# Banks for the maxima and the values, and the steps of the weight roundings, in a cross-attention stage

## The reference

```python
xn = _layernorm(x, ln1_w, ln1_b)              # ctx, 77 tokens, enters as the queries' side of the reference's names
q = latn @ Wq                                 # latents: 1024 tokens a batch, 16 heads of 64
kv = jnp.concatenate([xn, latn], axis=1) @ Wkv  # 77 + 1024 = 1101 keys and values
weight = jax.nn.softmax(einsum('bhld,bhnd->bhln', q * scale, k * scale), axis=-1)
out = einsum('bhln,bhnd->bhld', weight, v)    # then @ Wo, added to x
```

## Time and profile before

| | |
|---|---|
| runs of the kernel, median (lowest to highest) | 1946.68 us (1941.79 to 1953.57), 3 runs |
| the profiled execution, its own time | 1941.14 us |
| span of its trace, first to last instruction | 1939.4 us |
| granted TensorE clock, mean | 0.918 of full |
| TensorE busy | 1682.8 us |
| VectorE busy | 1233.6 us |
| GpSimd busy | 880.0 us |
| ScalarE busy | 698.5 us |

### The profile page before, as it was taken

The page is one execution under the profiler, slowest core; times in us unless marked ns, Lnnn a source line. Parts: engine busy times, 40 slices in busy tenths (PEclk is TensorE's granted clock), DMA queues, the critical chain, the costliest instruction groups (busy, mean ns, idle before and its releaser), DMA issues.

```text
span 1939.4 us, 46407 instructions
## 1 busy us (share of the span) xinstructions
PE 1682.8 (87%) x18226; PEld 1314.2 (68%) x18226; DVE 1233.6 (64%) x2531; ACT 698.5 (36%) x1295; POOL 880.0 (45%) x851
## 2 busy tenths in 40 slices
PE   1889999999998999999999727999999539999798
PEld 1677777777776777777777516777777425556587
DVE  8767767777775777767777742333675384346676
ACT  1344443444434344444444313444344201123122
POOL 4146655566551556655565524554454211112221
PEclk9899999999999999999999958999999756568699
DMA  8133433434421343443434191111211200000000
GB/s 202 34 88 87 121 92 86 99 87 121 102 77 33 90 99 87 121 97 81 99 91 112 41 394 59 59 51 45 73 40 32 77 0 1 1 1 1 33 12 33
DMA packets 67717, 148.43 MB, mean 77 GB/s; under 512 B 14779, under 2 KB 37619, under 8 KB 66996
## 3 DMA queue, kind: packets, MB, share of 16 engines
q1 hardware_dynamic: 63764, 135.20, 26.2%
q0 software_dynamic: 3744, 10.26, 1.4%
HBM read 57.85 MB, written 35.21 MB: 48 GB/s over the span
## 4 chain that ended last, share of the span: by engine, by line
PE 72%; DVE 13%; DMA 5%; issue 3%; ACT 2%; SPq 1%; POOL 1%; POOLq 0%; ACTq 0%; DVEq 0%
PE ps L1757 28%; PE ps L1853 9%; PE ps L1790 8%; PE ps L2020 7%; PE ps L1833 6%; PE ps L2110 6%; PE ps L1834 5%; DVE mxs L1203 4%; DMA KA<-K_l 4%; DVE Y L418 1%; SPq L585 1%; PE ps L1995 1%; PE ps L1860 1%; PE ps L2088 1%; DVE stats L399 1%
## 5 line engine op out<-in xcount | busy, mean ns | idle before, releaser
L756 POOL TENSOR_TENSOR PR<-PT 128x512 f16<-128x512 f32 (+1 forms) x416 | 441.6, 1073 | 442.1 <-ACT PT L966 441.9
L966 ACT ACTIVATE PT<-ps 128x512 f32<-128x512 f32 (+1 forms) x576 | 325.4, 596 | 382.9 <-PE ps L1834 382.8
L1853 PE MATMUL ps<-V_h,PT 128*128 128x65 f16 (+1 forms) x2304 | 319.8, 196 | 7.9 <-POOL PR L756 5.6
L1853 PE MATMUL ps<-V_l,PT 128*128 128x65 f16 (+1 forms) x2304 | 315.6, 194 | 0.0
L1853 PE MATMUL ps<-V_l,PR 128*128 128x65 f16 (+1 forms) x2304 | 314.0, 194 | 0.0
L1853 PE MATMUL ps<-V_h,PR 128*128 128x65 f16 (+1 forms) x2304 | 313.5, 193 | 0.0
L1203 DVE TENSOR_REDUCE mxs<-ps 128x1 f32<-128x736 f32 x256 | 236.2, 923 | 87.0 <-PE ps L1790 87.0
L1853 PEld LDWEIGHTS ps<-V_h,PT 128*128 128x128 bf16 (+1 forms) x2304 | 225.1, 98 | 97.9 <-issue 58.1
L1790 PE MATMUL ps<-KA,QA 128*128 128x368 f32 x768 | 214.6, 358 | 48.6 <-DVE mxs L1203 28.2
L1833 PE MATMUL ps<-QA,KA 128*128 128x512 f32 (+1 forms) x576 | 241.9, 420 | 15.6 <-ACT PT L966 10.8
L1834 PE MATMUL ps<-QB,KB 65*128 65x512 f32 (+1 forms) x576 | 229.2, 398 | 0.0
(11 more groups left out here) (354 smaller groups left out, 3745.6 us busy)
## 6 DMA issues: line engine op xcount, KB each, us to landing
QA<-Q_h SPq DMA_DIRECT2D x64, 256.0 KB, 4.6
latf<-wexp SPq DMA_DIRECT2D x32, 512.0 KB, 4.4
wsplit<-wst SPq DMA_DIRECT2D x32, 512.0 KB, 2.9
wx<-wsplit SPq DMA_DIRECT2D x8, 2048.0 KB
KA<-K_h SPq DMA_DIRECT2D x32, 275.5 KB, 3.1
KA<-K_l SPq DMA_DIRECT2D x32, 275.5 KB, 4.7
KB<-K_h SPq DMA_DIRECT2D x32, 275.5 KB, 5.7
QB<-Q_l SPq DMA_DIRECT2D x32, 256.0 KB, 5.5
```

The lines of the kernel that those rows point to most:

```text
L756: nc.gpsimd.tensor_tensor(PR[0:m, s % RING, :], PT[0:m, s % RING, :], upper(s)[0:m], ALU.subtract).then_inc(s_rem_pool, 1)
L966: nc.scalar.activation(PT[0:m, s % RING, :], score_banks[s % 2][0:m], ACT.Exp, scale=HD ** -0.5).then_inc(s_exp, 1)
L1853: mm = nc.tensor.matmul(pv_bank[:, q, :], p, v, start=(kt == 0 and q == 0 and k == 0), stop=(kt == KT - 1 and k == 3), skip_group_check=True)
```

## The change

- `value_bank` (new): in the second batch the values' jobs go round four banks, 5 and 6 and then 2 and 3; the waits on TensorE follow (a job waits for the one four before it). The first batch stays.
- Maxima of the next pair's first head: odd tiles put their second and third product into banks 5 and 6 (`two=True`, `pair`), even tiles into 3 and 4 as before; bank 2 stays single. A tile's second part waits for the second part of the tile two before. All three products stand ahead of the step's attend. At step 20 TensorE also waits until the shared banks are free of the keys' and queries' jobs.
- Roundings of the expert weights: high halves in steps 23 and 25 instead of 22 and 23, low halves in 26 and 28 instead of 25 and 26; in the next turn high in 1 and 3 instead of 0 and 1, low in 4 and 6 instead of 3 and 4.

```diff
--- before.py
+++ after.py
@@ -446,6 +446,11 @@
         def casts_before(b, i):
             return VJOBS + 5 + b * (CASTS * PAIRS + 2 + VJOBS) + CASTS * i
 
+        def value_bank(b, job, j):
+            if b > 0 and j % 4 >= 2:
+                return ps[:, j % 4, :]
+            return shared[(job + j) % 2]
+
         def first_qk_bank(j):
             return max_banks[:, j % 2 * HALF:j % 2 * HALF + HALF]
 
@@ -521,8 +526,8 @@
         WQK_AT, WO_SPLIT_AT = 7, 16
 
         WMAX_AT, WSCALE_AT = {15: 0, 29: 1}, {16: 0, 30: 1}
-        WHI_AT, WLO_AT = {22: 0, 23: 1}, {25: 0, 26: 1}
-        WHI_NEXT, WLO_NEXT = {0: 0, 1: 1}, {3: 0, 4: 1}
+        WHI_AT, WLO_AT = {23: 0, 25: 1}, {26: 0, 28: 1}
+        WHI_NEXT, WLO_NEXT = {1: 0, 3: 1}, {4: 0, 6: 1}
 
         def piece_halves(at, at_next, g, s):
 
@@ -939,7 +944,7 @@
                     if b > 0 and j == 0:
                         act.wait_ge(s_pv, STEPS * PAIRS * b + RING)
                     nc.scalar.activation(V["h"][0:m, kt, PAIRS * half:PAIRS * half + PAIRS, 0:HD],
-                                         shared[(job + j) % 2][0:m].rearrange("p (h d) -> p h d", d=HD), ACT.Identity,
+                                         value_bank(b, job, j)[0:m].rearrange("p (h d) -> p h d", d=HD), ACT.Identity,
                                          scale=vs[0:m, 0:1]).then_inc(s_cast, 1)
 
             for j in range(len(LATJOBS) - QK0_AT, 5):
@@ -1196,11 +1201,12 @@
             nc.vector.tensor_scalar(vs[:, 0:1], vs[:, 0:1], 16384.0, None, ALU.mult).then_inc(s_vs, 1)
             nc.vector.tensor_scalar(vs[:, 1:2], vs[:, 3:4], 1.0 / 16384.0, None, ALU.mult)
 
-            def max_tile(t, n):
+            def max_tile(t, n, two=False):
+                pair = 5 if two and t % 2 == 1 else 3
                 dve.wait_ge(s_mx, 2 * n + 1)
                 nc.vector.tensor_reduce(mxs[:, 0, t:t + 1], ps[:, 2, 0:MAXW], AX.X, ALU.max).then_inc(s_mxfree, 1)
                 dve.wait_ge(s_mx, 2 * n + 2)
-                nc.vector.tensor_reduce(mxs[:, 1, t:t + 1], ps[:, 3:5, 0:MAXW], AX.XY, ALU.max).then_inc(s_mxfree, 1)
+                nc.vector.tensor_reduce(mxs[:, 1, t:t + 1], ps[:, pair:pair + 2, 0:MAXW], AX.XY, ALU.max).then_inc(s_mxfree, 1)
 
             def max_join(n):
                 dve.wait_ge(s_mxfree, 2 * n + 2)
@@ -1218,7 +1224,7 @@
                     dve.wait_ge(s_cast, cast + j + 1)
                     heads = slice(PAIRS * half, PAIRS * half + PAIRS)
                     nc.vector.scalar_tensor_tensor(out=V["l"][0:m, kt, heads, 0:HD],
-                                                   in0=shared[(job + j) % 2][0:m].rearrange("p (h d) -> p h d", d=HD),
+                                                   in0=value_bank(b, job, j)[0:m].rearrange("p (h d) -> p h d", d=HD),
                                                    scalar=vs[0:m, 0:1], in1=V["h"][0:m, kt, heads, 0:HD],
                                                    op0=ALU.mult, op1=ALU.subtract).then_inc(s_jobfree, 1)
                     if b == 0 and half == 0 and kt < TB:
@@ -1286,7 +1292,7 @@
                                 dve.wait_ge(s_stackb[1], 32 * g + 32)
                             rest_qk(j, casts_before(b, i) + 2 + j + 1, bank(AWJOBS + j))
                         if M0_AT <= s < M0_AT + TB:
-                            max_tile(s - M0_AT, 16 * g + 16 + s - M0_AT)
+                            max_tile(s - M0_AT, 16 * g + 16 + s - M0_AT, two=True)
                         if s == M0_MAX:
                             max_join(16 * g + 24)
                         if s == M0_T:
@@ -1782,12 +1788,12 @@
                 if k >= QK0_AT:
                     project_qk(k - QK0_AT, 0, k - QK0_AT, first_qk_bank(k - QK0_AT))
 
-            def max_part(h, t, a, n):
-
-                pe.wait_ge(s_mxfree, 2 * n + a + 1)
+            def max_part(h, t, a, n, two=False):
+
+                pe.wait_ge(s_mxfree, 2 * n + a + 1 - (2 if two and a == 1 else 0))
                 q = QA[h][:, t * P:t * P + P]
                 for i in MAX_PARTS[a]:
-                    mm = nc.tensor.matmul(ps[:, 2 + i, 0:MAXW], q, KA[h][:, MAXC[i]:MAXC[i] + MAXW], start=True, stop=True)
+                    mm = nc.tensor.matmul(ps[:, 2 + i + (2 if two and a == 1 and t % 2 == 1 else 0), 0:MAXW], q, KA[h][:, MAXC[i]:MAXC[i] + MAXW], start=True, stop=True)
                 mm.then_inc(s_mx, 1)
 
             def max_tile(h, t, n):
@@ -1803,8 +1809,11 @@
                 for j in range(VJOBS):
                     kt, half = divmod(j, 2)
                     m = P if kt < TB else S
-                    pe.wait_ge(s_jobfree, job + j + 1)
-                    product(shared[(job + j) % 2][0:m],
+                    if b == 0 or j < 2:
+                        pe.wait_ge(s_jobfree, job + j + 1)
+                    elif j >= 4:
+                        pe.wait_ge(s_jobfree, job + j - 1)
+                    product(value_bank(b, job, j)[0:m],
                             [(lat[u][:, b, c, kt * P:kt * P + m], wv[v][:, c, HALF * half:HALF * half + HALF])
                              for c in range(NC) for u, v in RANDL]).then_inc(s_job, 1)
                     if b == 0 and half == 0 and kt < TB:
@@ -1886,9 +1895,11 @@
                         max_part(1, s - M1_AT, 0, 16 * g + 8 + s - M1_AT)
                     if nb is not None and M0_AT <= s < M0_AT + TB:
                         if s == M0_AT:
+                            pe.wait_ge(s_jobfree, job + AWJOBS + 5 + 2)
                             pe.wait_ge(s_stack[0], 64 * g + 128)
                             pe.wait_ge(s_maxrow, 2 * g + 2)
-                        max_part(0, s - M0_AT, 0, 16 * g + 16 + s - M0_AT)
+                        max_part(0, s - M0_AT, 0, 16 * g + 16 + s - M0_AT, two=True)
+                        max_part(0, s - M0_AT, 1, 16 * g + 16 + s - M0_AT, two=True)
                     if A_AT <= s < A_AT + 2:
                         if s == A_AT:
                             pe.wait_ge(s_norm, 4 * g + 2)
@@ -1908,8 +1919,6 @@
                                 pe.wait_ge(s_wqk, 2 * g + 4)
                             j = AWJOBS + s - QK_AT
                             project_qk(s - QK_AT, nb, job + j, bank(j))
-                        if M0_AT <= s < M0_AT + TB:
-                            max_part(0, s - M0_AT, 1, 16 * g + 16 + s - M0_AT)
                         if s == M0_T:
                             max_turn(2 * g + 2)
                 if nb is not None:
```

## The result

The changed kernel took 1906.23 us in the median of four executions (1883.77 to 1928.51), the kernel before 1944.24 us (1940.36 to 1953.57). The ratio is 0.969, 95% interval 0.963 to 0.975: faster. The prediction was 1924.8 us with 1899 to 1937, so the median lies under it by 18.6 us.

A forecast was written before the change was run, and what follows sets the result against it. TensorE, busy 87%, was taken to bound the kernel through its idle time. The terms -30.0 - 3.2 + 9.5 + 1.8 + 0 = -21.9 us gave 1919.2 from the profiled 1941.14, 1924.8 us at the median; range 1899 to 1937.

The forecast's parts named there:

- Maxima, -30.0: Steps 20 to 27: TensorE's four 0.50 us waits for VectorE's reduction go, 2.0 us a turn in 15 turns.
- rival c: TensorE waits for bank 2 or a late attend; half the maxima's gain stays away: -15, 1940 us; chance 0.12.
- Values, -3.2: Second batch, values on four banks: TensorE's gaps at 8 places go, 0.4 us each, 3.2 us saved.
- Seam, 14 x 0.68 = +9.5: Between two turns, GpSimd's earlier remainder delays VectorE's remainders: 0.68 us lost at each of 14 seams.
- Rival (a): VectorE goes first at one of the seam's two places: -0.16 us a seam, 1913 us; chance 0.17.
- Rival (b): No collision of GpSimd and VectorE at the seam: -0.94 us a seam, 1902 us; chance 0.16.
- Load and L1303, 0: Around step 29: the next weight piece lands later, VectorE's operation on it starts 0.5 us later, at no cost.
- Rival (d): Slower: the late load of the piece at step 29 becomes the bound; about 1959 us at 8.5 us load; chance 0.05.
- Last turn, +1.8: Turn without maxima of a next head: low half, load and remainders move back, +1.8 us (0 to 2.5).

The follow-up runs named there:

- the banks alone: Changed kernel with all four tables of roundings as before, so maxima and values alone: 1909.44 us, ratio 0.981.
- the first two tables alone: Kernel before with only the turn's first roundings moved (steps 23/25 and 26/28): median 1945.16 us, one execution at 1897.46.
- the mix: Changed kernel with the same turn's roundings back at 22/23 and 25/26, remainders of steps 34 and 35 on GpSimd: median 1901.91 us, one at 1858.82.

## Why the prediction was wrong

**Maxima, -30.0: right.** -1.97 us a turn, 32 waits left as forecast, VectorE fast enough (rival c fell).

**Values, -3.2: right**, -3.5 us between two kernels that differ in this alone, one profile of each.

**Seam, 14 x 0.68 = +9.5: right** in mechanism and size. The usual seam is longer by 9.24 - 8.56 = 0.68 us, to the hundredth, and the order of asking, worked out from the earlier trace rows, gave both ends of L1275. All 14 together are 10.7 us longer; four of the five long ones are those where the clock falls. Rival (a), one place won by VectorE, came in two of the 14 seams (8.50 and 8.41 us, the forecast for it was 8.56 - 0.16 = 8.40); in the three other profiles of this stage it came in two or three. The prediction had it as all or nothing. Rival (b), the seam that gains, is what a kernel shows that takes VectorE out of the two steps (7.63 us).

**Load and L1303, 0: right** as far as the runs show. It waits 0.3 us in the seam shown (0.5 forecast), and the usual seam is 9.24 us whether the load comes late or early (the kernel with only the next turn's tables). Rival (d) fell.

**Last turn, +1.8: undersized.** 53.21 to 56.08 us, +2.9, which includes up to 0.5 of scatter: six other profiles with the turn's own tables unmoved and its remainders on VectorE have 53.4 to 53.7 us. L1303 waits there for its load by 3.32 us, and the roundings' own tables cost as much alone (56.1):

```profile
1080.92 1.22 DVE L1303 TENSOR_REDUCE wtmp<-latf 128x1 f32<-128x1024 f32 x1 [3.32 <-DMA latf<-wexp]
```

**A missing term of the first attention, about +6.5 us.** The prediction took the granted clock as it was, and the profiled execution of the kernel before has no fall of it between 110 us and turn 15. That of the kernel after has falls in four seams of its 14 (behind turns 3, 5, 8 and 13, counted from 0) and in step 19 of turn 2. One of them, in the table of windows:

```profile
966.40:969.80 3.40, 2.11 (x36) 1.51 (x35) 2.64 (x3) 1.83 (x4) 1.69 (x2) 1.00 0.96 197
969.90:973.30 3.40, 3.40 (x33) 2.72 (x31) 1.52 (x4) 1.41 (x3) 2.20 (x2) 0.50 0.96 200
```

TensorE, which has just waited for both L1275, is busy 2.11 of 3.40 us, and then the clock is 0.50 for 3.4 us. All six profiles of kernels with the next turn's tables moved and steps 34 and 35 on VectorE have three to five such falls in their seams. The ten other profiles have none in a seam but where the batch changes, not even the one whose seam has a single wait of 0.8 us (products behind attend, 9.43 us). So the falls in the seams go with its two waits.

The fall in turn 2 does not. The kernel before with four products in second attention is the kernel before up to there, and its profile has falls in turn 2, around the change of batch and in turn 14, here that of turn 14:

```profile
1026.50:1029.90 3.40, 3.40 (x24) 2.84 (x24) 2.26 (x3) 0.04 (x1) 0.05 (x1) 0.51 0.15 31
```

Its first attention ends at 1115.3 us, that of the kernel before with ten products at 1113.6, where the execution that the prediction started from had 1111.8: it was the one of the three without any fall in turns 0 to 14. Against it the terms give -29.6 - 3.5 + 9.5 + 6.5 + 2.9 + 0.8 = -13.4 us, as measured. The 6.5 is not measured apart: it is what remains at the start of turn 15 (-17.1 us where the first three terms make -23.6); the 0.8 comes behind the last attend, where the clock is low for 6.8 us instead of 3.4. Between the means of the three profiles of this stage before and the four after, the shift is -15.8 us.

**The failing step** is the sum's silent one, a term put at nothing without a reason: that behind the first attention everything stays as long as it was. The prediction added its terms to the one profiled execution of before, without reading that the stage behind it ran 119.5 us at half clock, and that this could be otherwise. It came to 41.5 us in the profiled execution, and this happened in 5 of 16 in all. Had the clock stayed, the kernel would stand at about 1929 us, 4 us from the forecast and inside the range; the range had no case for it. That nearness is in part luck: at the same clock the change gives 15 to 19 us and not 21.9, as the last turn and the falls in the seams were undersized or missing. The Trainium skill, in its page TensorE: Matmul & The Clock Gate, Part 1: The HAM clock gate, says that the number of slow products at a kernel's start varies from run to run, and puts the loss from that ramp under 1% of a typical span. The first is like the two groups of times here; the second does not carry over to a stage in mid-kernel, where it was 41.5 of 1939 us, 2.1%.

**Still open:** why the changed kernel has the higher clock in 5 of 16 executions and the kernel before in 1 of 44. The kernels with the banks alone, with the maxima alone (in either order), with only the next turn's tables moved, with steps 34 and 35 on GpSimd and with four products never had it in the 4 to 6 executions of each, the roundings alone, the first two tables alone and the mix once in six. No single part shows a share clearly its own.

What the profiles do show is where the clock falls. In the kernel before the stage starts at 1608.30 and the fall comes at 1610.0, 1.7 us behind; in the kernel after the stage starts at 1595.63 and the fall has come at 1594.6, 1.0 us ahead. The row and the table of windows for the kernel before, and the latter for the one with the maxima alone, whose stage starts at 1579.60:

```profile
1608.30 0.42 PE L2110 MATMUL ps<-Q_h,KD_h 128*77 128x512 f32 x1 [2.25 <-issue]
```

```profile
1607.10:1610.00 2.90, 1.70 (x7) 0.91 (x8) 2.73 (x11) 0.18 (x1) 0.00 (x0) 1.00 0.00 0
```

```profile
1578.00:1731.60 153.60, 152.00 (x1012) 82.55 (x1012) 57.56 (x115) 30.18 (x51) 26.33 (x25) 0.50 0.00 1
```

All 13 profiles whose hole is open or half filled follow this. The three with the short low stretch (after, roundings alone, mix) have the fall 1.0 to 1.1 us ahead of the stage's first product, three with 123 to 154 us have it 1.2 to 1.6 us ahead, and seven with 119.5 us have it 1.4 to 1.8 us behind. So the length goes with the place of the fall; what sets that place was not tested.

## What to carry to other kernels

Look at the row of the granted clock before the sum: where a long stage runs at half clock behind a short hole of TensorE's, the stage is one term with two values, and which it takes can outweigh the change; fill the hole, as worked here, and compare kernels at the same clock. One profiled execution is not a baseline for falls of the clock either: take two or three. Give a change of several parts one kernel for each: here two parts were worth 32 us and the third took more than half of it back. Where VectorE and GpSimd shut each other out, as in these remainders, moving one of them earlier changed who waits and lost 0.68 us a seam; taking one engine out of the place gained 0.93.

## What was not expected of the hardware

- Second attention has two speeds in the same kernel: low for 6.8 us and then at 2.4 GHz, or low for 119.5 us (122.8 us in one profiled execution of another kernel here and 153.6 us in two), with TensorE shown busy for 98% of that time or more. Idle 2.25 us ahead of it, both occur; with 1.33 us idle behind four products it was the long one in the profile, and by their times in all four executions; with none idle the low stretch was absent in every profile taken (three kernels).
- Behind waits of 0.50 and 0.78 us one step apart, in a seam, the clock fell to 0.50 for 3.4 or 6.8 us in 4 of 14 seams, and in 3 to 5 of 14 in five more profiles. Behind the single wait of 0.68 us of the seam before it never fell outside the change of batch.
- Of a remainder on VectorE and one on GpSimd the one whose row begins first goes first, in the profile after even by 0.03 us: it takes 0.68 us on VectorE or mostly 1.0 to 1.2 us on GpSimd, and the other one about 1.5 us.
